# Output projection moved into the attention, head by head, on the chosen queries only

## The chip, the cores and the metric

One core of a Trainium2 chip runs the whole program in one launch. Its engines are TensorE (PE in the profile), VectorE (DVE), ScalarE (ACT), GpSimd (POOL) and SyncE (SP), which only issues DMAs. The metric is the device time of one execution in microseconds (us); less is better.

## The reference

The program is one transformer block with adaptive layer norm, on x of 4 batches of 2048 tokens with 512 features. The attention has 16 heads of 32 features, so there are 64 pairs of batch and head. Only the 409 queries of a head with the largest norm attend; all other token rows of that head are zero. What matters here:

```python
top_u = max(1, L // TOP_FACTOR)                       # 409 of 2048
_, top_idx = jax.lax.top_k(query_norms, top_u)
scores = jnp.einsum('bud,bld->bul', Q_sel, K) * scale
out_sel = jnp.einsum('bul,bld->bud', jax.nn.softmax(scores, axis=-1), V)
out_full = out_full.at[jnp.arange(BH)[:, None], top_idx].set(out_sel)   # zeros elsewhere
return out @ Wo.T + bo                                # per token: 512 -> 512
...
x = x + ga * attention(h)
h = layernorm(x) * (1 + cb) + sb
x = x + gb * ffn(h)      # 512 -> 1408 -> 512, both sides in blockwise FP4
```

## The kernel before

It runs in stages: `queries` and `keys_values` project the tokens and choose the queries (up to about 640 us), `attend` goes over the 64 heads (to about 1580 us), and `feed_forward` over 64 tiles of 128 tokens (to the end). There is no scheduler. Each engine has its program written out by hand as a list of steps with semaphore waits; in the middle each is a hardware loop (two heads or four tiles per turn), with the first and last turns written out.

In `attend`, a slot is one head on TensorE and has 8 steps k. Each step does `scores` (two 128x410 matmuls into one pair of PSUM banks), which ScalarE turns into exponentials; each odd step also does `weigh`, 8 fp32 matmuls with the values; each even step holds something smaller: a look for the row maxima of a coming head (`scores_for_max`), the transposes of queries (`turn_queries`), of maxima (`rows`) and of the output (`turn_output`). VectorE reduces the maxima and divides the output (`divide`). GpSimd, for each head, cuts the gathered queries into high and low halves (`cut_queries`), issues 4 indirect DMAs that gather the queries of the head two on, adds the bias bv, and issues 4 indirect DMAs (128, 128, 128 and 25 rows of 32 floats) that write the head's rows into the scratch tensor o_d (`scatter`). o_d has been filled with zeros before, a batch at a time.

In `feed_forward`, a tile's rows are loaded from o_d (a_in), transposed on TensorE (`turn_a`), split into f16 halves on ScalarE and VectorE (`high_of_a`, `low_of_a`), multiplied by Wo in 12 matmuls of 512 columns (`attention_out`), and taken with the bias bo on VectorE (`take_attention`). GpSimd then multiplies by ga and adds x (`residual`), VectorE and GpSimd normalise, modulate and quantise (`moments`, `normalise`, `modulate`, `quantise_h`, `scale_h`), and TensorE does the three products of the feed-forward with f16 halves (`gate_up`, `down`). `hidden_units`, `hidden_add` and `hidden_take` quantise the hidden 1408 values on VectorE, a tile behind. TensorE and VectorE work on three tiles at a time in a fixed order, `slot(t, ...)`.

Of the kernel before, what the change touches and what calls it, by code (L numbers as in the profile page):

```python
# [483 lines left out]
def keys_values(nc, keep, io, scratch, con, proj, h_hi, h_lo, early, ahead):  # L484
# [32 lines left out]
    with ExitStack() as stack:  # L517
# [5 lines left out]
        zeros = m.sb("zeros", [P, D], F32)  # L523
# [50 lines left out]
        bias_loaded, ones_set, zeros_set = keep.sem("bias_loaded"), keep.sem("ones_set"), keep.sem("zeros_set")  # L574
# [86 lines left out]
        with nc.Block() as block:  # L661
            @block.sync
            def _(sp):
# [53 lines left out]
                sp.dma_start(bv[:, :], io["bv"].unsqueeze(0).to_broadcast([P, D])).then_inc(bias_loaded, 16)  # L717
                for k in range(2):
                    sp.dma_start(nrm[k * BH:(k + 1) * BH, :], scratch["nrm"].rearrange("b h l -> (b h) l")[:, k * W:(k + 1) * W])\
                      .then_inc(nrm_loaded, 16)  # L720
# [5 lines left out]
                sp.wait_ge(zeros_set, 1)  # L726
# [5 lines left out]
                for s in range(BLOCKS):  # L732
# [16 lines left out]
                    if 1 <= s < 1 + PER_B:  # L749
                        sp.dma_start(o_blocks[s - 1], zeros[:, :].unsqueeze(1).to_broadcast([P, TB, D]))\  # L750
                          .then_inc(con["o_zeroed"], 16)
# [51 lines left out]
            def _(ve):  # L803
# [186 lines left out]
                ve.memset(v32[:, :, :, HD:VCOLS], 1.0).then_inc(ones_set, 1)  # L990
                ve.wait_ge(ones_set, 1)
                ve.sem_inc(v_done, TB)
                ve.memset(zeros[:, :], 0.0).then_inc(zeros_set, 1)
# [260 lines left out]
def attend(nc, keep, scratch, con, ffn, early, ahead, shared, banks, then):  # L1254
# [13 lines left out]
    ROWS_AT = 6  # L1268
    CHUNKS_AT = {0: ((1, 3), (1, 4)), 2: ((1, 5), (1, 6)), 4: ((2, 0),), 6: ((2, 1), (2, 2))}
    with ExitStack() as stack:  # L1270
# [9 lines left out]
        zeros = shared[:, at_o + QT * P:at_o + QT * P + D]  # L1280
# [3 lines left out]
        o_rows_of = [m.sb(f"o_rows{u}", [P, QT, HD], F32) for u in range(2)]  # L1284
        ps_max, ps_exp, ps_out, ps_misc = banks[0:2], *banks[2:5]

        o_pad, zeros_set = keep.sem("o_pad"), keep.sem("o_zeros_set")
# [10 lines left out]
        o_biased, o_stored = keep.sem("o_biased"), keep.sems("o_stored", 2)  # L1298
# [3 lines left out]
        o_rows = scratch["o"].rearrange("b l (h r) -> (b l h) r", r=HD)  # L1302
# [24 lines left out]
        with nc.Block() as block:  # L1327
            @block.sync
            def _(sp):

                f_front, f_run = then["sync"](sp, o_divided, o_stored)

                def load_k_max(h, u):
# [13 lines left out]
                def load_weights(k):  # L1347
                    part, w = divmod(k, 3)
                    if w < 2:
# [4 lines left out]
                def slot(i, u):  # L1354
# [3 lines left out]
                    if b + 1 < B and j < 8 and j % 2 == 0:  # L1358
                        sp.dma_start(o_blocks[b + 1, j // 2], zeros[:, :].unsqueeze(1).to_broadcast([P, TB, D])).then_inc(o_zeroed, 16)
# [5 lines left out]
                    if i == FRONT_IN:  # L1365
                        for v in range(2):
                            sp.wait_ge(o_stored[v], 16 * QT * H // 2)
                        f_front()

                for i in range(BH):  # L1370
                    if i == 4:
                        sp.wait_ge(zeros_set, 1)
                    slot(i, i % 2)
                f_run()
# [9 lines left out]
            def _(pool):  # L1384
                def scatter(h):
                    u = h % 2
                    pool.wait_ge(o_divided, h + 1)
                    pool.tensor_tensor(o_rows_of[u][:, :, :], o_rows_of[u][:, :, :],
# [3 lines left out]
                    if h % H == 0:  # L1392
                        pool.wait_ge(o_zeroed, 16 * (L // N) * (h // H + 1))
                    for t in range(QT):
                        n = rows_of(t, TOP)
                        pool.indirect_dma_start(o_rows, bass.IndirectOffsetOnAxis(ap=con["chosen"][0:n, t, h:h + 1], axis=0),  # L1396
                                                o_rows_of[u][0:n, t, :], None).then_inc(o_stored[u], 16)

                for h in range(BH):
# [4 lines left out]
                    if h >= 4:  # L1404
                        scatter(h - 4)
                f_constants, f_residual, f_modulate, f_scale_h, f_run = then["gpsimd"](pool)
                scatter(BH - 4)
                scatter(BH - 3)
# [4 lines left out]
                f_scale_h(0)  # L1413
                f_modulate(1, 0)
                scatter(BH - 2)
# [3 lines left out]
                scatter(BH - 1)  # L1419
# [928 lines left out]
```

## Time and profile before

| | |
|---|---|
| median of 3 runs | 3267.48 us (3266.4 to 3269.31) |
| the profiled execution's own time | 3266.15 us |
| its span, first to last instruction | 3264.3 us |
| TensorE busy | 3159.4 us (97%) |
| VectorE busy | 2544.5 us (78%) |
| ScalarE busy | 1143.1 us (35%) |
| GpSimd busy | 1562.5 us (48%) |

TensorE is busy nearly always, but its matmuls overlap in the records: a 512-column matmul is shown as 0.38 us and the next one starts 0.215 us after it. What a matmul costs is read from the distance between starts. Shares of busy time differ by stage, so each stage is looked at by itself.

### The profile page before, as it was taken

To read this page: it belongs to the slowest core of one execution; us is meant where nothing else is said; L and a number is where in the kernel's file an instruction comes from. 1 tells how busy PE (TensorE), PEld (TensorE's weight loads), DVE (VectorE), ACT (ScalarE), POOL (GpSimd) and SP (SyncE) were. 2 spreads that over 40 slices of the span, in tenths; PEclk is the share of its full clock that TensorE was granted. 3 is DMA by queue.
4 is the path that set the end of the run, shared out by engine and by line. 5 is a ranking of instruction groups with operands and counts; after the bars stand their busy time and mean duration, and the time that the engine had idled before them with its cause. 6 is when DMAs were issued, how large, how long until landed. Compare 5 with 4: busy or idle time off the path is not lost.

```text
span 3264.3 us, 49910 instructions
## 1 busy us (share of the span) xinstructions
PE 3159.4 (97%) x16684; PEld 1473.9 (45%) x16684; DVE 2544.5 (78%) x3769; ACT 1143.1 (35%) x1607; POOL 1562.5 (48%) x1420
## 2 busy tenths in 40 slices
PE   7998999899999999999999999999999999999998
PEld 3543454333333333333455555555555555555554
DVE  4657876566666666666789998998899999888995
ACT  6862323356666666665311111111111111111111
POOL 3432224266666666664544444444444444444442
PEclk9999999999999999999999999999999999999999
DMA  6856748655233343324110000110101000000000
GB/s 236 281 175 212 208 119 217 190 151 165 80 111 103 83 121 93 82 80 125 45 30 32 29 29 29 32 32 29 32 29 29 29 32 32 29 29 32 29 20 17
DMA packets 203480, 282.17 MB, mean 86 GB/s; under 512 B 59897, under 2 KB 115577, under 8 KB 202633
## 3 DMA queue, kind: packets, MB, share of 16 engines
q1 hardware_dynamic: 187016, 274.41, 27.8%
q0 software_dynamic: 16384, 6.76, 1.0%
q8 instruction: 43, 0.70, 0.1%
q14 instruction: 37, 0.30, 0.0%
HBM read 169.36 MB, written 111.70 MB: 86 GB/s over the span
## 4 chain that ended last, share of the span: by engine, by line
PE 74%; ACT 2%; DVE 2%; issue 1%; POOL 1%; DMA 0%; SPq 0%; ACTq 0%; POOLq 0%; DVEq 0%
PE bank L1648 12%; PE pair L2181 9%; PE pair L2183 9%; PE pair L2182 9%; PE pair L1637 7%; PE pair L1599 5%; PE bank L2203 4%; PE bank L2205 4%; PE bank L2204 4%; ACT shared L1540 2%; PE pair L2160 2%; PE pair L2162 2%; PE pair L2161 2%; PE bank L2193 1%; PE pair L2193 1%
## 5 line engine op out<-in xcount | busy, mean ns | idle before, releaser
L1435 DVE TENSOR_REDUCE top<-pair 128x1 f32<-128x1024 f32 x378 | 451.0, 1221 | 219.0 <-PE pair L1599 219.0
L1540 ACT ACTIVATE shared<-pair,p_bias 128x820 f32<-128x820 f32 x512 | 483.6, 945 | 369.7 <-PE pair L1637 369.6
L2181 PE MATMUL pair<-gu,xT_hi 128*128 128x512 f16 (+1 forms) x1536 | 555.0, 361 | 4.1 <-DVE bridge L1942 2.2
L2183 PE MATMUL pair<-gu,xT_lo 128*128 128x512 f16 (+1 forms) x1536 | 555.0, 361 | 0.0
L2182 PE MATMUL pair<-gu,xT_hi 128*128 128x512 f16 (+1 forms) x1536 | 555.0, 361 | 0.0
L1648 PE MATMUL bank<-shared,bridge 128*33 128x410 f32 x2048 | 404.8, 516 | 0.0
L1637 PE MATMUL pair<-q_exp,bridge 98*128 98x410 f16 x1024 | 267.6, 343 | 25.9 <-ACT shared L1540 25.4
L455 POOL DMA_INDIRECT q_sel<-q_d,chosen x256 | 245.8, 960 | 94.9 <-issue 79.0
L1396 POOL DMA_INDIRECT o_d<-o_rows,chosen x256 | 250.3, 978 | 81.5 <-issue 64.1
L2203 PE MATMUL bank<-dn,bridge 128*128 128x512 f16 x704 | 267.9, 381 | 0.0
L2204 PE MATMUL bank<-dn,bridge 128*128 128x512 f16 x704 | 267.8, 380 | 0.0
L2205 PE MATMUL bank<-dn,bridge 128*128 128x512 f16 x704 | 267.8, 380 | 0.0
L2113 ACT ACTIVATE silu<-pair 128x512 f32<-128x512 f32 (+1 forms) x128 | 69.6, 544 | 509.0 <-PE pair L2183 509.0
L1599 PE MATMUL pair<-bridge,q_max 96*128 96x512 f16 x756 | 209.0, 385 | 14.2 <-DVEq L1481 12.0
L2183 PEld LDWEIGHTS pair<-gu,xT_lo 128*128 128x128 f16 x1536 | 150.3, 98 | 153.9
L2181 PEld LDWEIGHTS pair<-gu,xT_hi 128*128 128x128 f16 x1536 | 150.3, 98 | 140.6 <-issue 3.5
L2182 PEld LDWEIGHTS pair<-gu,xT_hi 128*128 128x128 f16 x1536 | 150.3, 98 | 137.1
L2044 POOL TENSOR_SCALAR f_rstd<-f_mv 128x1 f32<-128x1 f32 x64 | 87.0, 1360 | 219.4 <-DVE f_mv L1915 219.4
L2107 ACT ACTIVATE xT_hi<-pair 128x512 f16<-128x512 f32 x64 | 38.2, 597 | 437.6 <-PE pair L2169 437.6
L1648 PEld LDWEIGHTS bank<-shared,bridge 128*33 128x33 f32 x2048 | 98.0, 110 | 204.2 <-issue 203.9
L1637 PEld LDWEIGHTS pair<-q_exp,bridge 98*128 98x128 f16 x1024 | 64.1, 97 | 264.7 <-ACT shared L1540 232.2
L2061 POOL TENSOR_TENSOR bridge<-bridge,q_scale 128x1408 f32<-128x1408 f32 x64 | 165.8, 2591 | 24.2 <-DVE bridge L1827 24.2
(280 smaller groups left out, 6036.9 us busy)
## 6 DMA issues: line engine op xcount, KB each, us to landing
bridge<-k_d SPq DMA_DIRECT2D x384, 128.0 KB, 3.3
v_d<-v SPq DMA_DIRECT2D x16, 1056.0 KB, 10.2
bridge<-v_d SPq DMA_DIRECT2D x64, 264.0 KB, 2.8
x<-in_x SPq DMA_DIRECT2D x16, 1024.0 KB, 8.6
q_d<-q SPq DMA_DIRECT2D x16, 1024.0 KB, 4.3
a_in<-o_d SPq DMA_DIRECT2D x64, 256.0 KB, 2.6
f_x<-in_x SPq DMA_DIRECT2D x64, 256.0 KB, 2.6
out<-shared SPq DMA_DIRECT2D x64, 256.0 KB, 2.0
```

Of the source, the lines that this page charges most:

```text
L1396: pool.indirect_dma_start(o_rows, bass.IndirectOffsetOnAxis(ap=con["chosen"][0:n, t, h:h + 1], axis=0), o_rows_of[u][0:n, t, :], None).the ...
L1435: ve.tensor_reduce(top[:, t, half:half + 1], ps[:, :, :].rearrange("p a n -> p (a n)"), AX.X, ALU.max, negate=True).then_inc(max_done, 1)
L1540: act.activation(p32[k % PB][:, :, :], ps_exp[:, :, 0:NQ], ACT.Exp, bias=con["p_bias"][:, 0:1], scale=scale).then_inc(p_done, 1)
L1599: last = pe.matmul(ps[:, s, :], q_max[u][:, t * P:(t + 1) * P], k_max[u][:, at:at + 512], start=True, stop=True)
L1637: last = pe.matmul(ps_exp[:, s, 0:NQ], k_exp[u][:, at:at + P], q_exp[u][:, :], start=True, stop=True)
L1648: last = pe.matmul(ps_out[at:at + VCOLS, 0:NQ], v_tok[u][:, t, :], p32[k % PB][:, s, :], start=k == 0, stop=k == STEPS - 1)
L2181: pe.matmul(o, xT_hi[:, c, :], w_hi[:, c, c0:c0 + n], start=c == 0, stop=False)
L2182: pe.matmul(o, xT_hi[:, c, :], w_lo[:, c, c0:c0 + n], start=False, stop=False)
L2183: last = pe.matmul(o, xT_lo[:, c, :], w_hi[:, c, c0:c0 + n], start=False, stop=c == KC - 1)
L2203: pe.matmul(ps_d[:, :], hT_hi[:, c, :], w_hi[:, c, :], start=c == 0, stop=False)
L2204: pe.matmul(ps_d[:, :], hT_hi[:, c, :], w_lo[:, c, :], start=False, stop=False)
L2205: last = pe.matmul(ps_d[:, :], hT_lo[:, c, :], w_hi[:, c, :], start=False, stop=c == FC - 1)
```

## The change

- In `attend`, each head's output is projected at once. After `divide`, GpSimd adds bv and cuts the result into f16 parts high, low, high (`cut_output`); TensorE transposes them (`turn_back`, 4 matmuls), VectorE copies them out (`take_back`), and TensorE multiplies by the 32 rows of Wo of that head, stacked as high, high, low (`project`, 4 matmuls with 96 rows of contraction and 512 columns). ScalarE scales the 4 results into SBUF (`take_rows`). They lie where dn[0], a half of the down weights, comes later.
- GpSimd's 4 indirect DMAs per head now add rows of 512 floats to whole token rows of o_d. Two heads can choose the same token, so the first of a head waits until all four of the head before have landed. The heads' steps trail: `divide` of a head is one slot behind TensorE's head, its `cut_output` too, its projections two and three slots behind.
- SyncE loads the head's rows of Wo (3 small DMAs, `load_wo`). o_d is filled with bo in place of zeros.
- In `feed_forward`, a_in is only loaded: `turn_a`, `high_of_a`, `low_of_a`, `attention_out` and `take_attention` are gone, and `residual` starts from a_in. `low_of_x` of the next tile moves ahead of `take_down`, and `turn_x` of the next tile into `down`. dn[0] is loaded after the last accumulating DMA has landed.

```diff
             def _(pool):
-                def scatter(h):
-                    u = h % 2
+                def scatter(h, tiles):
+                    for t in tiles:
+                        n = rows_of(t, TOP)
+                        pool.wait_ge(o_taken, h * QT + t + 1)
+                        if t == 0:
+                            for k in range(QT):
+                                need(pool, o_stored[k], 16 * h)
...
+                        pool.indirect_dma_start(o_rows, bass.IndirectOffsetOnAxis(ap=token[0:n, t, h:h + 1], axis=0),
+                                                o_tile[t][0:n, :], None, compute_op=ALU.add).then_inc(o_stored[t], 16)
+
+                def cut_output(h):
                     pool.wait_ge(o_divided, h + 1)
...
+                    need(pool, o_back, h)
+                    pool.tensor_copy(o_split[:, :, :].rearrange("p t (k r) -> p t k r", k=3)[:, :, 0:3:2, :],
+                                     o_div[:, :, :].unsqueeze(2).to_broadcast([P, QT, 2, HD])).then_inc(o_high, 1)
+                    pool.wait_ge(o_high, h + 1)
+                    pool.tensor_tensor(o_split[:, :, HD:2 * HD], o_div[:, :, :], o_split[:, :, 0:HD], ALU.subtract).then_inc(o_cut, 1)
+
+                def outputs(h):
+                    if 0 <= h - 2:
+                        scatter(h - 2, range(1, QT))
+                    if 0 <= h < BH:
+                        cut_output(h)
+                    if 0 <= h - 1 < BH:
+                        scatter(h - 1, range(1))
...
             def _(act):
+                def take_rows(h, t, bank):
+                    n = rows_of(t, TOP)
+                    act.wait_ge(o_proj, h * QT + t + 1)
+                    need(act, o_stored[t], h * 16)
+                    act.activation(o_tile[t][0:n, :], bank[0:n, :], ACT.Copy, scale=1.0 / (W_UP * O_UP)).then_inc(o_taken, 1)
...
             def _(pe):
+                def project(h, u, t, bank, loaded, taken):
+                    n = rows_of(t, TOP)
...
+                    pe.matmul(bank[0:n, :], oT[u][:, t * P:t * P + n], wo_head[u][:, :], start=True, stop=True).then_inc(o_proj, 1)
...
         def residual(t, t4, b):
-            hold(pool, y_done, t + 1, pool_held)
-            pool.tensor_tensor(y[:, :], y[:, :], vec["ga"][:, b, :], ALU.mult).then_inc(ga_done, 1)
+            pool.wait_ge(fa_in[t4 % 2], in_turn(t, t4))
+            if has(t, -1):
+                hold(pool, x2_done, t, pool_held)
+            pool.tensor_tensor(y[:, :], a_in[t4 % 2][:, :], vec["ga"][:, b, :], ALU.mult).then_inc(ga_done, 1)
...
         def slot(t, t4, b1, b2, b_z):
             hidden(t, 1)
-            if has(t, 2):
-                low_of_a(t + 2)
             if has(t, 1):
                 quantise_h(t + 1)
             hidden(t, 2)
             hidden_units(t)
+            if has(t, 1):
+                low_of_x(t + 1)
             if has(t, -2):
                 take_down(t - 2, b_z)
```

TensorE in the attention loop, from the scores of an odd step to those of the next one, first before and then after (`wo_head,oT` is a projection, `o_split` the transposes of `turn_back`, `shared,bridge` the weighing):

```order
L1637 MATMUL pair<-q_exp,bridge 128x410 x2
L1648 MATMUL bank<-shared,bridge 33x410 x2
L1648 MATMUL bank<-shared,bridge 33x410 x2
L1637 MATMUL pair<-q_exp,bridge 128x410 x2
L1599 MATMUL pair<-bridge,q_max 128x512 x2
L1603 MATMUL pair<-bridge,q_max 26x512 x4
L1637 MATMUL pair<-q_exp,bridge 128x410 x2
```

```order
L1701 MATMUL pair<-q_exp,bridge 128x410 x2
L1712 MATMUL bank<-shared,bridge 33x410 x2
L1744 MATMUL bank<-wo_head,oT 128x512
L1712 MATMUL bank<-shared,bridge 33x410 x2
L1701 MATMUL pair<-q_exp,bridge 128x410 x2
L1661 MATMUL pair<-bridge,q_max 128x512 x2
L1665 MATMUL pair<-bridge,q_max 26x512 x4
L1734 MATMUL bank<-ident,o_split 96x128 x3
L1734 MATMUL bank<-ident,o_split 96x26
L1701 MATMUL pair<-q_exp,bridge 128x410 x2
```

A projection stands between the two halves of each odd step's weighing, four to a head, and the four transposes at the end of step 2.

GpSimd in the attention, one head and the start of the next, before and after (`q_sel<-q_d` gathers the queries, `o_d<-` writes or adds the output rows):

```order
L465 CAST q_split<-q_sel 128x4x64
L468 TENSOR_TENSOR q_split<-q_sel,q_split 128x4x32
L455 DMA q_sel<-q_d,chosen 128x32 x3
L455 DMA q_sel<-q_d,chosen 26x32
L1388 TENSOR_TENSOR o_rows<-o_rows,bv 128x128
L1396 DMA o_d<-o_rows,chosen 131072x32 x4
```

```order
L465 CAST q_split<-q_sel 128x4x64
L468 TENSOR_TENSOR q_split<-q_sel,q_split 128x4x32
L455 DMA q_sel<-q_d,chosen 128x32 x3
L455 DMA q_sel<-q_d,chosen 26x32
L1415 DMA o_d<-dn,token 8192x512 x3
L1420 TENSOR_TENSOR o_div<-o_div,bv 128x128
L1425 CAST o_split<-o_div 128x4x2x32
L1428 TENSOR_TENSOR o_split<-o_div,o_split 128x4x32
L1415 DMA o_d<-dn,token 8192x512
```

The number of DMAs is the same; three of an older head now stand ahead of the addition of bv and one behind the cut, and that one waits for the three.

VectorE in the feed-forward loop, over the boundary between two tiles, before and after (`bank,shared` is `take_down`, `xT_lo` is `low_of_x`, `pair,bo` is `take_attention`, the 1408 wide ones are `hidden_add`):

```order
L1812 SCALAR_TENSOR_TENSOR bridge<-bridge,q_inv 128x1408
L1956 SCALAR_TENSOR_TENSOR bridge<-bank,shared 128x512
L1895 TENSOR_TENSOR xT_lo<-pair,xT_hi 128x512
L1948 SCALAR_TENSOR_TENSOR bridge<-bank,bridge 128x512
L1908 SCALAR_TENSOR_TENSOR bridge<-pair,bo 128x512
L1948 SCALAR_TENSOR_TENSOR bridge<-pair,bridge 128x512
L1819 TENSOR_SCALAR bridge<-bridge 128x1408
```

```order
L1918 SCALAR_TENSOR_TENSOR bridge<-bridge,q_inv 128x1408
L1999 TENSOR_TENSOR xT_lo<-pair,xT_hi 128x512
L2047 SCALAR_TENSOR_TENSOR bridge<-bank,shared 128x512
L2039 SCALAR_TENSOR_TENSOR bridge<-bank,bridge 128x512
L2039 SCALAR_TENSOR_TENSOR bridge<-pair,bridge 128x512
L1925 TENSOR_SCALAR bridge<-bridge 128x1408
```

`take_attention` has gone, and `low_of_x` and `take_down` have changed places.

## Rows read from the trace of the kernel before

**Rows 1.** Busy time by stretch: length, PE, PEld, DVE, ACT, POOL, clock, DMA share.

```profile
700.00:1510.00 810.00, 789.50 (x4413) 269.00 (x4413) 553.79 (x964) 500.88 (x623) 505.36 (x619) 1.00 0.37 106
1700.00:3100.00 1400.00, 1400.00 (x7312) 733.64 (x7310) 1261.24 (x1559) 228.10 (x430) 667.24 (x485) 1.00 0.10 30
```

**Rows 2.** Instructions in order of time, PE, attention: start us, length us, [idle before].

```profile
1070.88 0.47 PE L1585 MATMUL bank<-ident,q_split 128*96 128x128 f16 x4
1071.29 1.04 PE L1599 MATMUL pair<-bridge,q_max 96*128 96x512 f16 x4
1072.16 0.52 PE L1637 MATMUL pair<-q_exp,bridge 98*128 98x410 f16 x2
1072.61 1.57 PE L1648 MATMUL bank<-shared,bridge 128*33 128x410 f32 x8
1074.12 0.52 PE L1637 MATMUL pair<-q_exp,bridge 98*128 98x410 f16 x2
...
1075.75 0.52 PE L1637 MATMUL pair<-q_exp,bridge 98*128 98x410 f16 x2 [0.35 <-ACT shared L1540]
...
1085.20 0.47 PE L1585 MATMUL bank<-ident,q_split 128*96 128x128 f16 x4
```

**Rows 3.** The same of GpSimd, attention.

```profile
1069.08 0.98 POOL L1396 DMA_INDIRECT o_d<-o_rows,chosen  x1 [0.30 <-issue]
1070.37 0.97 POOL L1396 DMA_INDIRECT o_d<-o_rows,chosen  x1 [0.30 <-issue]
...
1072.58 0.40 POOL L465 CAST q_split<-q_sel 128x256 f16<-128x256 f32 x1
...
1077.63 0.89 POOL L455 DMA_INDIRECT q_sel<-q_d,chosen  x1 [0.30 <-issue]
1081.44 0.45 POOL L1388 TENSOR_TENSOR o_rows<-o_rows,bv 128x128 f32<-128x128 f32 x1 [2.92 <-DVE o_rows L1470]
```

**Rows 4.** DMA issues, whole span: count, KB each, median us to landing.

```profile
a_in<-o_d SPq DMA_DIRECT2D x64, 256.0 KB, 2.6
...
out<-shared SPq DMA_DIRECT2D x64, 256.0 KB, 2.0
```

**Rows 5.** In order of time, PE, feed-forward.

```profile
2401.16 0.38 PE L2160 MATMUL pair<-wo_hi,aT_hi 128*128 128x512 f16 x1
...
2403.75 0.60 PE L2193 MATMUL pair<-ident,bridge 128*128 128x128 f32 x4
...
2414.88 0.60 PE L2154 MATMUL pair<-ident,a_in 128*128 128x128 f32 x4
...
2427.21 0.38 PE L2160 MATMUL pair<-wo_hi,aT_hi 128*128 128x512 f16 x1
```

**Rows 6.** In order of time, VectorE, feed-forward.

```profile
2402.09 0.68 DVE L1956 SCALAR_TENSOR_TENSOR bridge<-bank,shared 128x512 f32<-128x512 f32 x1
...
2405.63 1.22 DVE L1819 TENSOR_SCALAR bridge<-bridge 128x1408 int32<-128x1408 int32 x1
...
2408.76 1.62 DVE L1823 TENSOR_TENSOR bridge<-bridge 128x1408 f32<-128x1408 f32 x1
...
2417.09 0.69 DVE L1805 TENSOR_REDUCE q_amax<-f_h 128x32 f32<-128x512 f32 x1
...
2427.80 0.68 DVE L1956 SCALAR_TENSOR_TENSOR bridge<-bank,shared 128x512 f32<-128x512 f32 x1
```

**Rows 7.** In order of time, GpSimd, feed-forward.

```profile
2402.86 1.27 POOL L2067 TENSOR_TENSOR shared<-x,bridge 128x512 f32<-128x512 f32 x1 [4.21 <-DVE bridge L1956]
2404.83 1.27 POOL L2036 TENSOR_TENSOR bridge<-bridge,vec_ga 128x512 f32<-128x512 f32 x1 [0.71 <-DVE bridge L1908]
2406.17 1.80 POOL L2040 TENSOR_TENSOR x<-f_x,bridge 128x512 f32<-128x512 f32 x1
...
2415.78 1.27 POOL L2050 TENSOR_TENSOR f_h<-f_h,vec_sb 128x512 f32<-128x512 f32 x1 [0.18 <-POOL f_h L2048]
```

**Rows 8.** VectorE near the end, where GpSimd is idle.

```profile
3212.46 0.88 DVE L1819 TENSOR_SCALAR bridge<-bridge 128x1408 int32<-128x1408 int32 x1
```

**Rows 9.** ScalarE, a copy of 512 columns out of PSUM.

```profile
2409.65 0.60 ACT L2113 ACTIVATE silu<-pair 128x512 f32<-128x512 f32 x1 [4.66 <-PE pair L2183]
```

More of the change, by code:

```diff
@@ L1418, in _ @@
                 f_modulate(2, 0)
-                scatter(BH - 1)
+                scatter(BH - 2, range(1, QT))
+                scatter(BH - 1, range(QT))
                 f_run()
@@ L1594, in scores_for_max @@
                     need(pe, max_done, h * CH + c - 1)
+                    if c == 1 and (not isinstance(h, int) or h >= 4):
+                        pe.wait_ge(o_taken, (h - 4) * QT + 1)
                     ps = ps_max[(u + c) % 2]
@@ L1738, in feed_forward @@
     res = late[0:2]
-    (ps_w, t0), (g0, u0), (g1, u1) = ((pair[:, 0, :], pair[:, 1, :]) for pair in banks[0:3])
+    (_, t0), (g0, u0), (g1, u1) = ((pair[:, 0, :], pair[:, 1, :]) for pair in banks[0:3])
     ps_d, t1 = banks[3][:, :], banks[4][:, :]
@@ L1868, in slot @@
                 load_vector(5, "gb")
-        def scattered():
-            for u in range(2):
-                sp.wait_ge(stored[u], 16 * QT * BH // 2)
+                for k in range(QT):
+                    sp.wait_ge(stored[k], 16 * BH)
+                sp.dma_start(ffn["dn"][0][:, :, :], scratch["dn"][0]).then_inc(con["f_in"], 16)
         def last():
@@ L1960, in slot @@
             if at(t, 0):
-                take_attention(2)
-                hidden(0, 0)
                 moments(2, 2)
@@ L1965, in slot @@
                 hidden(0, 1)
-                low_of_a(3)
                 hidden(0, 2)
@@ L1983, in slot @@
                 ve.wait_ge(vec_in["gb"], 16)
-            else:
-                low_of_x(t)
             if has(t, -2):
                 low_of_hidden(t - 2, 0)
-            if has(t, 1):
-                take_attention(t + 1)
             if has(t, -2):
@@ L2023, in run @@
             drive(ve, slot, last)
-        return low_of_a, take_attention, moments, normalise, quantise_h, low_of_x, run
+        return hidden, moments, normalise, quantise_h, low_of_x, run
     def gpsimd(pool):
@@ L2131, in slot @@
             gate(t, 1)
-            if at(t, 0):
-                high_of_a(3)
-            elif has(t, 2) and not at(t, 1):
-                high_of_a(t + 2)
             gate(t, 2)
@@ L2195, in turn_hidden, with down @@
             last.then_inc(t_turned, 1)
-        def down(t):
+        def down(t, turn=None):
             need(pe, z_done, t)
+            if at(t, 0):
+                pe.wait_ge(con["f_in"], 6 * 16)
             for k, (c0, n) in enumerate(T2_CHUNKS):
+                if k == 2 and turn is not None:
+                    turn_x(turn)
                 pe.wait_ge(t_lo, turn2_at(t, k) + 1)
@@ L2220, in slot @@
             if at(t, 2):
-                attention_out(3)
-                pe.wait_ge(divided, BH)
+                pe.wait_ge(projected, BH * QT)
             if has(t, -2):
                 turn_hidden(t - 2, 0)
-            if has(t, 1) and not at(t, 2):
-                attention_out(t + 1)
             if has(t, -2):
@@ L2232, in slot @@
             gate_up(t, 1)
-            if has(t, 2):
-                turn_a(t + 2, t4 + 2)
             gate_up(t, 2)
             if has(t, -2):
-                down(t - 2)
+                down(t - 2, t + 1 if has(t, 1) else None)
         def last():
```

275 lines of the change are left out of this document (155 added, 120 removed).

## The prediction

> **What bounds the kernel now.** I first read the busy time by stretch. The attention and the feed-forward are both TensorE's: 789.5 of 810 us and 1400 of 1400 us [rows 1]. Then the instructions in order of time, for the length of a turn. In the attention a head takes 1085.20 - 1070.88 = 14.32 us [rows 2], with one wait of 0.35 us for an exponential; VectorE and ScalarE stand at 68% and 62%, GpSimd at 62% and more, since about 0.3 us lie between its issues [rows 1, 3]. In the feed-forward a tile takes 2427.21 - 2401.16 = 26.05 us [rows 5]. There VectorE is at 90% [rows 1]: 1261.24/1400 of 26.05 us is 23.5 us. So the change adds to the engine that bounds the attention, and takes from the engine that bounds the feed-forward, but a second engine stands right behind it there.
>
> **What the attention pays.** TensorE, per head:
> - 4 projections. Four 512-column matmuls took 1072.16 - 1071.29 = 0.87 us, so one is 0.22 us. Each stands inside the fp32 weighing, and going from f16 into fp32 costs something: the two 410-column scores take 0.45 us before the weighing [rows 2], where 2 x 410 columns at 0.87/2048 us each would be 0.35 us. With 0.09 to 0.10 us for it, a projection costs 0.31 us, four 1.25 us. Bounds: 0.22 us each (0.87), and 0.40 us each if the fp32 pipeline drains at both sides (1.6).
> - 4 transposes of `turn_back`. Their like took 1071.29 - 1070.88 = 0.41 us. They stand at the end of step 2, just where TensorE waited 0.35 us for the exponential [rows 2], so 0.02 to 0.06 us are left.
>
> That is 1.27 us, a head of 15.6 us. ScalarE gets 4 copies of 0.60 us [rows 9]: 62% of 14.32 is 8.9 us, plus 2.4 is 11.3 of 15.6 us. They come right behind an odd step's exponential, and the next scores are then still 0.75 us of weighing away, so they delay no exponential. VectorE gets one copy of 410 columns, under 0.7 us by its 512-column operations [rows 6], on 9.8 us. Both are hidden while TensorE is the bound.
>
> GpSimd has the same 8 indirect DMAs, at 1070.37 - 1069.08 = 1.29 us each, and two more operations, like its cast of 0.40 us [rows 3]. 8 x 1.29 + 0.9 (cut of the queries) + 1.6 (bias and cut of the output, with gaps) is 12.9 us of 15.6. The new wait is the thing: the first scatter of a head waits until the four of the head before have landed. Behind it in GpSimd's queue stand the next cut of the queries and four gathers, then three scatters. From the start of a head's last scatter round to the next one's: its issue 1.0 us, landing, the first scatter 1.29, cut and gathers 1077.63 - 1072.58 + 1.28 = 6.3, two scatters 2.6: 11.2 us plus the landing. While it is under 15.6 - 11.2 = 4.4 us from the end of the issue, TensorE never sees it. No row shows an accumulating DMA. 256 KB read from o_d landed in 2.6 us and 256 KB written took 2.0 us [rows 4]; the accumulate must read and write, so 2.0 us is the floor and 4.6 us one after the other, and above that there is no row: sharing the queues with the loads of keys could double it, to 9 us. I take 3.5 us, between the two sums, also because the last of the four has only 25 rows. The issue itself may be longer than 1.29 us too, as each row needs another read; at 1.6 us the free landing shrinks to about 3 us.
>
> The Trainium skill (DMA: Bandwidth & Descriptors, Anatomy of one DMA) gives 2.0 us plus bytes over 436 GB/s for a DMA issued from GpSimd; an estimate by it is 2.6 us for 128 rows of 2 KB, which would leave the wait hidden. No run here shows it for an accumulating one.
>
> About 62 slots carry this: 62 x 1.27 = +79 us (54 to 100 by the bounds, with the wait hidden).
>
> **What the feed-forward gives back.** TensorE loses 12 matmuls, 2403.75 - 2401.16 = 2.6 us, and four transposes, under 0.6 us [rows 5]: it needs 23.0 us a tile. If that were all, 58 tiles would give 177 us. It isn't, since VectorE and GpSimd form a ring that takes nearly as long as before. I follow it from `take_down` to `take_down`, 2427.80 - 2402.09 = 25.71 us in this tile [rows 6]:
> - `low_of_a` goes, 0.68 us. But the next operation, q_amax at 2417.09, started when GpSimd's last modulation ended (2415.78 + 1.27 = 2417.05) [rows 6, 7]. VectorE now waits there instead; nothing is gained.
> - `take_attention` goes, and with it GpSimd no longer waits for it (0.71 us idle ahead of 2404.83). GpSimd's three additions now follow each other from 0.77 us after `take_down`. VectorE comes to `hidden_add` at 2.06 us instead of 3.54 us, into these. The two engines do not run such operations together: L1819 took 1.22 us here and 0.88 us where GpSimd is idle [rows 6, 8], and GpSimd's addition 1.80 us, where its like takes 1.27. Taken in turn: 0.77 + 1.27 + 1.27 + 0.76 + 1.15 + 0.76 = 5.98 us from `take_down` to L1823. Before it was 2408.76 - 2402.09 = 6.67 us, but that held `low_of_x` (0.60 us), which now comes at the other end of the ring.
> - So the ring is 5.98 + (25.71 - 6.67) + 0.60 = 25.6 us; with the handovers as short as the trace has them, 25.4. I take 25.5, against 26.05: 0.55 us a tile, times 58 is -32 us.
>
> Bounds: if GpSimd's additions and `hidden_add` fell beside each other for nothing, the ring would lose 0.7 to 0.9 us more, 24.6 us (-84 us); if they fell worse, 26.05 (0). The rule behind it is in the Trainium skill (SBUF — State Buffer, two separate sides): the port pair that VectorE and GpSimd share is an exclusive lock held for the whole instruction. By this rule the trace agrees, with 1.22 against 0.88 us, and it speaks against the change: work that is taken off VectorE next to GpSimd's additions turns partly into waiting for them.
>
> **The rest.** Between the stages GpSimd now issues 4 x 4 scatters among the first tiles' modulations, with waits for landings; TensorE was short of work there already. 0 to 20 us, I take 5. The load of the down weights waits for the last scatter, but its first use comes two tiles (some 29 us) after the last projection. The load of bo and the smaller SyncE steps hide behind loads that run anyway: 0 to 2, I take 0.
>
> Sum, against the execution profiled: 3266.15 + 79 - 32 + 5 = 3318. The median shown is 1.3 us above that execution, which is nothing here.
>
> **Rivals.**
> 1. GpSimd's ring binds the attention: slower still. Place: the wait for the four landings ahead of a head's first scatter; it decides from a landing of 4.4 us on (3 us if an issue takes 1.6 us), and each us more costs 62 us. At 6 us: 17.2 us a head, 3318 + 99 = 3417; at 8 us some 3540. For it: the loads of keys share the engines at 37% [rows 1]; against it: 25 rows only in the last scatter, and 4.6 us as the sum of a read and a write.
> 2. The feed-forward falls to TensorE's 23.0 us: faster. It needs VectorE's waits for GpSimd to vanish. 3266 + 79 - 177 + 5 = 3173. Against it: 23.5 us of VectorE's own work less 1.3 is 22.2, and the waits for GpSimd's reciprocal root and modulations, which stay, are 2 us on top.
> 3. The two cancel: projections at 0.22 us and a ring of 24.6 to 25 us. 3266 + 55 - 60 to -84 + 5 = 3242 to 3266.
>
> **Chances.** The forecast as worked out (3285 to 3350): 0.52. Rival 1: 0.25. Rival 2: 0.08. Rival 3: 0.15, of which half within 0.2% (6.5 us, about what a measurement here can tell from none). So faster 0.16, same 0.08, slower 0.76. The range reaches from rival 3's lower part to rival 1 with a landing of 6 us: 3245 to 3420; the forecast's own is 3285 to 3350.
>
> **What would show it.** Right: a head of 15.4 to 15.7 us with projections spaced 0.31 us inside the weighing, GpSimd idle ahead of the first scatter; a tile of 25.2 to 25.7 us, TensorE waiting in it for low_of_x or hidden, q_amax waiting over 1 us for GpSimd, L1819's successor at 1.5 us or more. Wrong: TensorE waiting in the attention for ScalarE's copies or GpSimd (rival 1), or a tile of 23 us (rival 2).

## The result, and the profile after

The changed kernel takes 3469.0 us (median of 4 runs, 3464.34 to 3475.03), the kernel before 3268.23 us beside it: a ratio of 1.0619 (1.0605 to 1.0632), 201 us slower. The profiled execution has a span of 3466.3 us, against 3264.3: 202.0 us more, which the traces divide as follows. The bounds are instructions that both kernels have: the transposes of a head's output in TensorE's timeline (L1659 before, L1725 after) and q_amax<-f_h on VectorE, once a tile.

| stretch | before, us | after, us | difference | the prediction had |
|---|---|---|---|---|
| up to head 0's output | 678.0 | 674.5 | -3.5 | 0 |
| head 0 to head 59 (59 heads) | 844.8 | 1045.3 | +200.5 | +79 (62 heads) |
| head 59 to tile 3 | 113.3 | 143.3 | +30.0 | +5 |
| tile 3 to tile 63 (60 tiles) | 1562.4 | 1536.4 | -26.0 | -32 (58 tiles) |
| tile 63 to the end | 65.8 | 66.8 | +1.0 | 0 |

First the page of the changed kernel: the span, the queue that the indirect transfers use (packets, MB, share of 16 engines), and the costliest lines that are new.

```profile
span 3466.3 us, 50118 instructions
PE 3179.1 (92%) x16172; PEld 1385.0 (40%) x16172; DVE 2527.9 (73%) x3706; ACT 1266.6 (37%) x1799; POOL 1792.8 (52%) x1548
q0 software_dynamic: 41984, 57.03, 11.9%
L1415 POOL DMA_INDIRECT o_d<-dn,token x256 | 400.4, 1564 | 275.0 <-DMA o_d<-dn,token 125.7
L455 POOL DMA_INDIRECT q_sel<-q_d,chosen x256 | 246.7, 964 | 94.2 <-issue 59.4
```

The scatter that adds takes GpSimd 1564 ns to issue, the gather beside it 964. The same stretches as in [rows 1], and the attention's as before:

```profile
700.00:1510.00 810.00, 760.42 (x3899) 233.42 (x3898) 467.51 (x818) 506.19 (x680) 550.45 (x584) 0.96 0.65 137
1900.00:3300.00 1400.00, 1291.49 (x6564) 647.55 (x6565) 1240.85 (x1475) 211.02 (x383) 702.82 (x494) 1.00 0.10 31
```

TensorE is no longer busy all the time in either. In the attention its granted clock is 0.96 where it was 1.00, and the DMA engines' share of busy time has gone from 0.37 to 0.65.

Now TensorE in order of time, a head without a wait. It answers to [rows 2], where eight fp32 matmuls stood in one piece:

```profile
704.93 0.50 PE L1725 MATMUL bank<-ident,shared 97*128 97x97 f32 x4
...
705.89 0.88 PE L1712 MATMUL bank<-shared,bridge 128*33 128x410 f32 x4
706.70 0.39 PE L1744 MATMUL pair<-wo_head,oT 96*128 96x512 f16 x1
707.02 0.88 PE L1712 MATMUL bank<-shared,bridge 128*33 128x410 f32 x4
707.84 0.52 PE L1701 MATMUL pair<-q_exp,bridge 98*128 98x410 f16 x2
...
721.05 0.50 PE L1725 MATMUL bank<-ident,shared 97*128 97x97 f32 x4
```

This head is 721.05 - 704.93 = 16.12 us. From the weighing's start to the next score it is 707.84 - 705.89 = 1.95 us; before it was 1074.12 - 1072.61 = 1.51 us [rows 2]. A projection costs 0.44 to 0.45 us, of which 0.32 are its own distance (706.70 to 707.02) and 0.12 lie in the two halves of the weighing, 0.81 and 0.82 us instead of 1.51 for both.

But the heads are not all 16.12 us. Their mean is 1045.3 / 59 = 17.72. GpSimd in order of time shows why:

```profile
1069.27 1.62 POOL L1415 DMA_INDIRECT o_d<-dn,token  x1 [0.30 <-ACT dn L1594]
1071.20 1.57 POOL L1415 DMA_INDIRECT o_d<-dn,token  x1 [0.30 <-issue]
1073.07 1.47 POOL L1415 DMA_INDIRECT o_d<-dn,token  x1 [0.30 <-issue]
...
1078.85 1.59 POOL L1415 DMA_INDIRECT o_d<-dn,token  x1 [2.85 <-DMA o_d<-dn,token]
...
1085.48 0.90 POOL L455 DMA_INDIRECT q_sel<-q_d,chosen  x1 [0.31 <-issue]
1086.68 1.62 POOL L1415 DMA_INDIRECT o_d<-dn,token  x1 [0.30 <-issue]
1088.61 1.57 POOL L1415 DMA_INDIRECT o_d<-dn,token  x1 [0.30 <-issue]
1090.48 1.46 POOL L1415 DMA_INDIRECT o_d<-dn,token  x1 [0.30 <-issue]
...
1096.40 1.60 POOL L1415 DMA_INDIRECT o_d<-dn,token  x1 [3.00 <-ACT dn L1594]
```

A scatter stands 1.9 us before the next (1.29 in [rows 3]). From a head's first scatter to the end of its last is 1090.48 + 1.46 - 1078.85 = 13.1 us, then comes the landing: 1078.85 - (1073.07 + 1.47) = 4.3 us. This is one turn; in the 51 turns of the steady part the first piece is 13.1 us each time, and the second goes from 3.4 to 6.6. In 34 turns a landing ends it (4.5 us on average), in the other 17, but for two, ScalarE's copy of a projected row tile (4.9 us), as in the last row above. 13.1 + 4.5 = 17.6 us is longer than TensorE's 16.12, and everything that hangs on a landing hands the wait on. ScalarE's copy into the row tile waits for the head before to land; TensorE's transposes of the next queries, in the bank that this copy empties, wait for ScalarE:

```profile
1075.11 0.60 ACT L1594 ACTIVATE dn<-bank 128x512 f32<-128x512 f32 x1 [2.73 <-DMA o_d<-dn,token]
```
```profile
1075.76 0.51 PE L1645 MATMUL bank<-ident,q_split 128*96 128x128 f16 x4 [1.53 <-ACT dn L1594]
```

TensorE's waits for these copies add up to 60 us in the 59 heads. That is not all of the 94 us by which the heads exceed TensorE's own (1045.3 less 59 x 16.12). In 14 of the 59 the granted clock fell as well, to a mean of 0.84 to 0.92 over the head, and 30 us of their length lie neither in the 16.12 nor in their waits. The drop comes behind a long wait. In the head that starts at 1029.35 us TensorE waits 2.96 us, and then stands at 0.50, the lower of its two levels (1.2 GHz, not 2.4):

```profile
1040.25 0.51 PE L1645 MATMUL bank<-ident,q_split 128*96 128x128 f16 x4 [2.96 <-ACT dn L1594]
```
```profile
1042.00:1044.00 2.00, 2.00 (x6) 0.30 (x5) 0.69 (x1) 0.94 (x1) 0.96 (x1) 0.50 0.00 0
```

GpSimd's turns average 17.72 us, as long as the heads, and the turns that end with a landing need 17.6, so the ring sets the pace. What TensorE lost to the clock can have added little to it: for the most part it lies in time that TensorE would otherwise have waited.

In the feed-forward a tile is 25.61 us. VectorE in one of them, against [rows 6]:

```profile
2400.90 0.69 DVE L1911 TENSOR_REDUCE q_amax<-f_h 128x32 f32<-128x512 f32 x1 [1.40 <-POOL f_h L2136]
2401.62 1.83 DVE L1914 TENSOR_SCALAR q_scale<-q_amax 128x32 f32<-128x32 f32 x1
...
2414.28 1.96 DVE L1925 TENSOR_SCALAR bridge<-bridge 128x1408 int32<-128x1408 int32 x1
2416.28 1.84 DVE L1927 TENSOR_SCALAR bridge<-bridge 128x1408 f32<-128x1408 f32 x1
```

q_amax waits 1.40 us for GpSimd's modulation, and L1925 takes 1.96 us beside GpSimd's additions, where its predecessor took 1.22, and 0.88 alone [rows 6, 8]. TensorE waits three times in that tile, for xq, for xT_lo (1.02 us) and for hidden; these are two:

```profile
2412.36 0.66 PE L2254 MATMUL pair<-ident,bridge 128*128 128x128 f32 x4 [1.02 <-DVE xT_lo L1999]
...
2424.29 0.32 PE L2242 MATMUL pair<-gu,xT_hi 128*128 128x384 f16 x1 [0.59 <-DVE bridge L2033]
```

Between the stages, from head 59 to tile 3, TensorE waits 36.1 us where it waited 10.3 before. 14.7 us of it are for ScalarE's copies of projected rows (dn), 5.7 for oT, the copy that VectorE makes of the turned output; these two waits are new:

```profile
1779.67 0.88 PE L1725 MATMUL bank<-ident,shared 97*128 97x97 f32 x4 [5.68 <-DVE oT L1506]
...
1824.78 0.60 PE L1744 MATMUL bank<-wo_head,oT 96*25 96x512 f16 x1 [10.50 <-ACT dn L1594]
```

In the second ScalarE itself waited 10.51 us for a scatter to land, and GpSimd had issued that scatter at 1818.99 us, behind tile 2's residual and modulation.

### The profile page after: what moved, and what is told of

The parts are those of the page before. It is cut to its first block, busy times and chain, and to the rows that moved or that the text cites. A ratio compares the mean times of both kernels' runs of the same rounds, so it can differ in the third digit from the quotient of the medians.

```text
span 3466.3 us, 50118 instructions
## 1 busy us (share of the span) xinstructions
PE 3179.1 (92%) x16172; PEld 1385.0 (40%) x16172; DVE 2527.9 (73%) x3706; ACT 1266.6 (37%) x1799; POOL 1792.8 (52%) x1548
## 3 DMA queue, kind: packets, MB, share of 16 engines
q0 software_dynamic: 41984, 57.03, 11.9%
## 4 chain that ended last, share of the span: by engine, by line
DVE 24%; POOL 20%; issue 13%; PE 13%; DMA 8%; ACT 2%; POOLq 0%; SPq 0%; DVEq 0%; ACTq 0%
DMA o_d<-dn,token 8%; POOL o_d L1415 5%; POOL q_sel L455 5%; DVE q_scale L1914 3%; PE bank L1712 3%; DVE bridge L1927 3%; DVE q_amax L1911 3%; POOL f_rstd L2130 3%; DVE bridge L1925 2%; POOL f_h L2134 2%; POOL f_h L2136 2%; PE pair L1701 2%; PE pair L1661 1%; DVE q_inv L1916 1%; DVE q_xn L1918 1%
## 5 line engine op out<-in xcount | busy, mean ns | idle before, releaser
L1415 POOL DMA_INDIRECT o_d<-dn,token x256 | 400.4, 1564 | 275.0 <-DMA o_d<-dn,token 125.7
L1712 PE MATMUL bank<-shared,bridge 128*33 128x410 f32 x2048 | 468.3, 538 | 0.0
L1661 PE MATMUL pair<-bridge,q_max 96*128 96x512 f16 x756 | 223.2, 391 | 17.8 <-DVEq L1523 12.1
L2141 POOL TENSOR_TENSOR q_xq<-q_xn,q_scale 128x512 f32<-128x512 f32 x64 | 68.8, 1075 | 227.9 <-DVE q_xn L1933 227.9
```

The costliest lines, as they stand in the source:

```text
L1712: last = pe.matmul(ps_out[at:at + VCOLS, 0:NQ], v_tok[u][:, t, :], p32[k % PB][:, s, :], start=k == 0, stop=k == STEPS - 1)
```

## Experiments

The stretches named below are those of the table. Each experiment ran on one chip together with the kernel before, and its ratio is to that. e1 to e8 fell on chips where the kernel before takes 3266 to 3267 us; the later ones where it took longer, of which more under e10.

### e1 and e2: what the accumulate costs

e1 leaves out the addition and writes the rows plainly, e2 leaves out half of each row.

```diff
-   o_tile[t][0:n, :], None, compute_op=ALU.add)          # e1
+   o_tile[t][0:n, :], None)
-   o_rows = scratch["o"].rearrange("b l d -> (b l) d")   # e2
+   o_rows = scratch["o"].rearrange("b l (k d) -> (b l k) d", k=2)
-   o_tile[t][0:n, :], None, compute_op=ALU.add)
+   o_tile[t][0:n, 0:D // 2], None, compute_op=ALU.add)
```

> The 256 indirect DMAs that add head rows into the token rows write them instead (same rows, same bytes, same waits; so what is loaded at the end is not the sum). Theory A (the accumulate makes GpSimd's ring too long: issue every 1.93 us instead of 1.29 us, landing some 4.5 us): the issue falls back to 1.29 us, the landing to 2 to 3 us, the ring to about 14 us, under TensorE's 16.12 us a head. Then every head takes 16.12 us and about 100 us go: 3360 to 3380 us. Rival B (the ring is long because the key loads share the DMA queues, accumulate or not): the landing stays above 4 us and at most 30 us go, 3440 us or more. Rival C (the longer heads come from the granted clock or from ScalarE's copies, not from the scatters): no change, 3469.

> The accumulating DMAs move 256 of each row's 512 numbers (the same count of rows, half the bytes; the other half of the sum is left out). If the cost of the accumulate is per row (a descriptor and a read each), the issue stays at 1.9 us spacing and the landing falls by less than 1 us: 3430 to 3469 us. If it goes by bytes, the landing falls by 1.5 to 2 us: the ring is 15.5 us and under TensorE's 16.12, 3360 to 3400 us.

e1: 3362.7 us, ratio 1.0297 (1.0280 to 1.0314): 106 us less than the changed kernel. Heads 0 to 59 take 949.5 us, 16.09 each. e2: 3383.6 us, 1.0361 (1.0344 to 1.0378), 85 us less, heads of 16.33 us. Three rows say what happened, the first of e1's page:

```profile
L1415 POOL DMA_INDIRECT o_d<-dn,token x256 | 252.7, 987 | 173.3 <-ACT dn L1594 106.0
```

and two of GpSimd in e2:

```profile
1002.50 1.46 POOL L1415 DMA_INDIRECT o_d<-dn,token  x1 [0.30 <-issue]
...
1006.74 1.59 POOL L1415 DMA_INDIRECT o_d<-dn,token  x1 [1.32 <-DMA o_d<-dn,token]
```

A plain write of the same rows is issued in 987 ns. With half the bytes the accumulate is issued as slowly as before (1564 ns mean), but lands 1006.74 - 1003.96 = 2.8 us after the issue instead of 4.3. So the bytes don't set the issue, and the landing falls with them. The rows don't set the issue either: the fourth scatter of a head has 25 rows and takes 1.46 us, the others have 128 and take 1.57 to 1.62. Nearly all of it is a price for each DMA. Theory A holds; its rivals B and C are out, since the addition alone was removed and all heads fell to TensorE's length at a granted clock of 1.00. Of e2's two answers the first was right on the issue, though not on its reason, and the second on the landing and the time.

### e3 and e4: the ring, and the place of the projections

```diff
-                    if 0 <= h - 2:                        # e3, e4
-                        scatter(h - 2, range(1, QT))
+                    if 0 <= h - 2:
+                        scatter(h - 2, range(QT))
                     if 0 <= h < BH:
                         cut_output(h)
-                    if 0 <= h - 1 < BH:
-                        scatter(h - 1, range(1))
-                            weigh(i, u, k - 3, in_turn(i, u, 0))   # e4 only
-                            project_in_turn(i, u, k)
+                            project_in_turn(i, u, k)
+                            weigh(i, u, k - 3, in_turn(i, u, 0))
                             weigh(i, u, k - 2, in_turn(i, u, 0))
```

> A head's first scatter is moved on GpSimd from behind the cut of the output to stand directly ahead of the other three, so that the landing of the four passes beside the cuts and the gathers and not in a wait. Theory A: GpSimd's turn is then 4 x 1.93 + 4 x 1.29 + about 2.5 = 15.4 us with no landing in it, TensorE's 16.12 us bounds every head: 3360 to 3380 us. Rival D (the indirect DMAs are held up in the queues themselves, so that GpSimd only waits elsewhere): less than 40 us go.

> As the one before, and each projection on TensorE is moved from between the two fp32 weighings of a step to ahead of both, behind the f16 scores. Theory A (a projection costs 0.45 us in the place it has: 0.22 us of columns and 0.23 us for leaving and entering fp32 once more): TensorE's head is 15.2 us; GpSimd's 15.4 us is then about as long: 3300 to 3330 us. Rival E (the 0.23 us belongs to the projection wherever it stands): as the one before.

e3: 3371.0 us, 1.0321 (1.0304 to 1.0338). The same operations with the same waits, in another order, and the heads are 16.12 us one like the other (949.5 us for 59); 98 us of the 201 are gone. So a wait goes away when GpSimd has other issues to make meanwhile, and rival D is out. The granted clock is back as well. Its stretch as in [rows 1], and below it e4's:

```profile
700.00:1510.00 810.00, 809.51 (x4322) 256.58 (x4321) 513.25 (x902) 564.36 (x755) 610.57 (x653) 1.00 0.68 149
```
```profile
700.00:1510.00 810.00, 806.41 (x4505) 286.13 (x4503) 537.21 (x946) 564.61 (x785) 636.39 (x680) 1.00 0.74 155
```

e4: 3334.2 us, 1.0210 (1.0193 to 1.0227), heads of 15.42 us. Ahead of the weighing, behind the f16 scores, a projection costs (15.42 - 14.32) / 4 = 0.28 us at most, in the middle of it 0.45. Theory A had 15.2 us for TensorE and 15.4 for GpSimd. The 15.42 are TensorE's own: in all of the 59 heads it waits for 3.0 us in total.

### e5 to e8: a remedy that was none

```diff
-        ve.tensor_scalar(sc[:, :], am[:, :], 1.0 / 6.0, 1e-12, ALU.mult, ALU.max).then_inc(step, 1)   # e5, e6, e7, e8
+        ve.scalar_tensor_tensor(out=sc[:, :], in0=am[:, :], scalar=1.0 / 6.0, in1=tiny[:, 0:1].to_broadcast([P, nb]),
+                                op0=ALU.mult, op1=ALU.max).then_inc(step, 1)
...
-                f_residual(2, 2, 0)                                            # e8
-                f_modulate(2, 0)
                 scatter(BH - 2, range(QT))
+                f_residual(2, 2, 0)
+                f_modulate(2, 0)
```

> The changed kernel with one VectorE instruction in another form: L1914 (q_scale<-q_amax, 128x32 and 128x88) is a scalar_tensor_tensor with a constant as second operand instead of a tensor_scalar with two numbers. In the trace of the changed kernel the 128x32 one takes 1.83 us wherever GpSimd's L2147 (2.58 us) runs, and 0.18 us elsewhere. Theory F (the feed-forward is bounded by the ring of VectorE and GpSimd, and this is a wait for GpSimd inside it): the tile falls from 25.61 us by about 1.6 us to 24.0, times 60: 3370 us (3360 to 3385). Rival G (TensorE is the bound again, or VectorE waits for GpSimd a few operations later instead): tile 25.3 us or more, 3450 to 3469 us.

> The same edit in the kernel before. There TensorE has no idle time in a tile of 26.04 us. If TensorE bounds it, nothing changes but the transition: 3255 to 3267 us. If VectorE and GpSimd bounded it in truth: 24.4 us a tile, about 3170 us.

> The changed kernel with the scatters together, the projections first, and q_scale unlocked. By the sums so far: 3334 from the first two, less 97 us of theory F: 3237 us (3225 to 3250), under the kernel before. If theory F fails, 3320 or more.

> As the one before, and between the stages GpSimd issues the scatters of head 62 ahead of tile 2's residual and modulation, not behind them. TensorE waited 6.89 us there for ScalarE, which waited for these to land. If that wait is what makes the transition long: 5 to 8 us less than the one before. If another wait takes its place (tile 2's quantisation comes later by the four issues, 7.5 us): the same or up to 5 us more.

e5: 3470.9 us, 1.0623 (1.0602 to 1.0645), tile 25.66 us: nothing. Theory F's remedy failed, but not as rival G had it either. The row of e5:

```profile
2402.04 1.84 DVE L1915 SCALAR_TENSOR_TENSOR q_scale<-q_amax,f_tiny 128x32 f32<-128x32 f32 x1
```

The other form stands still just as long, 1.84 us, to the end of GpSimd's scaling of the hidden row (2401.24 + 2.59 = 2403.83 us). The Trainium skill says that itself (SBUF — State Buffer, Who interferes with whom): a VectorE instruction with two inputs in SBUF contends with a GpSimd one that reads SBUF, and tensor_reduce never does. The trace agrees in both: q_amax, a reduction that starts at 2401.32 us beside the same GpSimd operation, keeps its 0.69 us.

e6 (the kernel before with the edit): 3267.7 us, 1.0001 (0.9991 to 1.0010), as TensorE's bound wants it, though after e5 it could show nothing else. e7 is e4 with this edit, e8 is e7 with head 62's scatters moved ahead of tile 2's work on GpSimd. e7: 3336.5 us and e8: 3335.5 us, both as e4. In e8 TensorE's longest wait for ScalarE's copy is 3.99 us instead of 5.49, and its wait for tile 2's xT_lo 4.62 instead of 2.42: the one took the place of the other.

### e9 and e10: the feed-forward's ring

```diff
             if has(t, 1):                       # GpSimd; e9, e10
+                gated(t + 1, t4 + 1, b1)        # y = a_in * ga, no longer inside residual
             if has(t, -3):
                 result(t - 3, t4 + 1)
...
-            if has(t, -1):                      # GpSimd; e10
-                scale_hidden(t - 1)
             if has(t, 1):
                 scale_h(t + 1)
+            if has(t, -1):
+                scale_hidden(t - 1, t4 + 1)
...
-            hidden_units(t)                     # VectorE; e10: q_amax, q_scale, q_inv,
-            low_of_x(t + 1)                     # then low_of_x, then the scaling L1918
+            hidden_units(t, t4, lambda: low_of_x(t + 1))
```

> The kernel with the scatters together and the projections first (e4, 3334 us), and in the feed-forward GpSimd's multiplication by ga (L2122, 1.27 us) is taken from behind the final addition (L2153) to ahead of it, where GpSimd stood idle for 4.8 us. Theory H (the tile is a ring in which VectorE's L1925 and L1927 stand still while GpSimd's three additions and multiplications run): they wait 1.0 us less, the tile falls from 25.61 to 24.6 (24.3 to 24.9), times 60: 3275 us (3255 to 3290). Rival I (the wait moves to the next place, as with q_scale in e5): tile 25.5 or more, 3325 us or more.

> As the one before, and GpSimd scales the hidden row (L2147, 2.58 us) behind scale_h instead of ahead of it, with low_of_x on VectorE ahead of the scaling L1918 of 1408 columns and two buffers for the hidden q_scale. Then q_amax is followed by q_scale at once and GpSimd's 2.58 us lie beside VectorE operations that did not wait in the traces (L1911, L1999). Theory H: 1.65 us less of standing still, but TensorE's own 23.5 us a tile is the floor: tile 23.6 to 24.2 us, 3215 to 3245 us, under the kernel before. Rival I: the tile stays at that of the run before.

e10 also gives the hidden q_scale a second buffer, which the lines above leave out. The tile fell to 24.76 us in e9 and 24.09 us in e10, as theory H had it; rival I is out. Four VectorE rows of e10:

```profile
2405.06 1.68 DVE L1913 TENSOR_SCALAR q_scale<-q_amax 128x88 f32<-128x88 f32 x1
...
2411.27 1.07 DVE L1927 TENSOR_SCALAR bridge<-bridge 128x1408 int32<-128x1408 int32 x1
...
2422.69 0.69 DVE L1909 TENSOR_REDUCE q_amax<-f_h 128x32 f32<-128x512 f32 x1 [1.40 <-POOL f_h L2140]
2423.41 0.18 DVE L1913 TENSOR_SCALAR q_scale<-q_amax 128x32 f32<-128x32 f32 x1
```

The small q_scale is back at 0.18 us (1.83 in the changed kernel) and the first operation of `hidden_add`, on 1408 columns, at 1.07 (1.96). But the hidden q_scale now stands still, 1.68 us where it took 0.21: a part of the wait moved. TensorE is busy for 1347.65 of 1400 us in that stage, where the changed kernel had 1291.49.

The times were 3377.3 us (1.0156, 1.0140 to 1.0171) and 3340.0 us (1.0048, 1.0035 to 1.0061), not the 3275 and 3215 to 3245 expected: there the kernel before took 3323.4 us, and heads 0 to 59 of the new version 1006 us where e4 had 912.

### e11 to e17: other chips

> The kernel of e10 again. In e10's call the kernel before itself took 3323 us instead of 3267, and heads of the attention 16.9 us where e4 had 15.42 at the same instructions. If that belongs to the chip, e10's tile of 24.09 us gives here, beside a kernel before of 3267 us, 3334 - 60 x (25.61 - 24.09) = 3243 us (3230 to 3255), ratio 0.990 to 0.996. If the longer heads are caused by the edits in the feed-forward (which lie behind the attention), it is 3330 us or more again.

> The kernel of e4 again, beside e11 on one chip, so that the difference of the two is the feed-forward's edits alone: e11 plus 60 x 1.52 = 91 us (80 to 100).

e11: 3339.2 us, 1.0037 (1.0024 to 1.0049). e12, which is e4 again: 3437.4 us, 1.0330 (1.0308 to 1.0353), with heads of 17.23 us, in a kernel that ran with 15.45 before. So the longer heads do not come from the edits but from where and when the kernel ran, and the feed-forward's edits are worth 98 us (80 to 100 expected). The attention of this version is hit harder there than that of the kernel before. The chip alone need not be it: e9 and e10 ran on chip 7, with 3323.4 us for the kernel before, and e13 to e15 on chip 7 too, with 3301.2.

> The version of e10 and e11, and on VectorE the moments, normalisation and quantisation of tile 0 stand behind the copy of head 61's turned output (take_back in head 63's turn) and not ahead of head 63's turn. TensorE waited 4.0 us in e4 and 5.7 us in the changed kernel for that copy (oT L1506). Theory J (VectorE's place in tile 0 makes that wait): it goes, the passage from head 59 to tile 3 is 3 to 6 us shorter than in e15. Rival K: tile 0 comes later by as much and TensorE waits for xT_lo instead: within 2 us of e15.

> The kernel before, unchanged, for its trace on this chip. If the chip is like the first: 3264 to 3270 us with heads of 14.32 us. If it is the one of the last two calls: about 3324 us, and the 57 us stand in the attention (heads of 15.2 us, 0.9 us more, with ScalarE waiting once a head), the tile at 26.04 us.

> The version of e10 and e11. On a chip like the first: 3234 to 3245 us, ratio 0.990 to 0.994. On the other chip: 3340 us, ratio 1.004.

The edit of e13 moves four steps in VectorE's program (f_moments(0, 0) to f_moments(1, 1)) from the end of head 62's turn to behind take_back of head 63's. e13: 3341.8 us, 1.0127 (1.0108 to 1.0145), e15: 3330.1 us, 1.0087 (1.0073 to 1.0102). The wait for oT went and one of 12.31 us for ScalarE's exponential came a few steps on; the passage from head 59 to tile 3 took 145.4 us against 137.9. The version without this edit has 132.5, 141.4, 137.9 and 141.2 us there in its four traces (e10, e11, e15, e16), so single traces differ by 9 us and say no more than this: nothing was gained. Theory J failed, and K, which had it within 2 us and with a wait for xT_lo, is not shown either. e14 took 3297.8 us, with heads of 14.87 us instead of 14.32 and the tile at 26.04. Its attention, to be read beside [rows 1]:

```profile
700.00:1510.00 810.00, 764.08 (x4248) 259.28 (x4244) 535.83 (x929) 482.86 (x599) 491.00 (x599) 1.00 0.36 103
```

> The version of e10, e11 and e15. On a chip where the kernel before takes 3267 us: heads of 15.4 us, tiles of 24.1 us, 3235 to 3250 us, ratio 0.990 to 0.995. On a chip where it takes 3300 us or more: ratio 1.004 to 1.009 as so far.

> The changed kernel with only the projections moved ahead of both weighings; GpSimd's order is left. TensorE's own head is 0.7 us shorter. If the ring (13.1 us plus a landing of 4.5 us = 17.6 us) bounds every head, at most 10 us go. If TensorE's 16.12 us bounds the heads between the waits, as the heads of exactly 16.12 us in the changed kernel suggest, part of the 59 x 0.7 = 41 us goes: 15 to 30 us, ratio to the kernel before 1.053 to 1.058.

e16: 3333.3 us, 1.0102 (1.0085 to 1.0119), on a chip where the kernel before took 3299.1 us. e17: 3498.0 us, 1.0607 (1.0589 to 1.0625), heads of 18.20 us. That is not shorter than the ring's 17.6. But the changed kernel itself was not run there, and even e16, with its scatters together, has heads of 17.07 us, so e17 proves nothing; e1 and e3 do.

On a chip like the first the best version would be e4 less 60 x (25.61 - 24.09) = 91 us, 3243 us, 0.7% under the kernel before. That is an estimate, not measured; measured four times (e10, e11, e15, e16), always where the kernel before took 3299 us or more, it was 0.4 to 1.0% slower. No version measured here beats the kernel before.

## Why the prediction was wrong

- **The step that failed** is "While it is under 15.6 - 11.2 = 4.4 us ..., TensorE never sees it": GpSimd's ring was put at 11.2 us plus a landing, and the wait at nothing. It was +94 us above TensorE's own head (200.5 less 59 x 1.80), and (17.72 - 15.6) x 59 = 125 us above the forecast's. The landing was not far off, 4.5 us against 3.5 and inside the bounds. The issue was: 1.29 us was taken over from a plain scatter, 1.9 was measured, and the fallback named (1.6) was still too short. The four scatters make the 11.2 us 13.1, which leaves 16.12 - 13.1 = 3.0 us for a landing of 4.5. Neither error alone would have done much: 13.1 + 3.5 = 16.6 and 11.2 + 4.5 = 15.7 us, against 16.12. Rival 1 named this place and mechanism, with 0.25; the sign that it gave for itself, TensorE waiting for ScalarE's copies, is what the trace shows. But its sums let only the landing grow, and its 3417 us at a landing of 6 us falls short for that reason. No term stood for the clock either: 60 of the 94 us are TensorE's waits and 30 lie in the 14 heads in which its clock fell behind one. e1 and e3 take away both together and can't part them. e3 takes away the wait and leaves the dearer issue, and gives back 98 us; e1 takes away the dearer issue and landing, and gives back 106.
- **Projections on TensorE**: 0.31 us each was right for the distance to the next matmul (0.32) and wrong for the cost, 0.45. The working had only the way from f16 into fp32; that the weighing's halves on both sides become longer (0.12 us) was left out. The bounds had 0.40 "if the fp32 pipeline drains at both sides"; even this was passed. The head of a TensorE without waits is 16.12 us, not 15.6: 59 x 1.80 = +106 us, against 59 x 1.27 = 75. e4 shows that the place costs it.
- **`turn_back`, ScalarE, VectorE in the attention**: hidden, as said. ScalarE's copies did come into the chain, but as carriers of the landing.
- **The feed-forward**: 25.61 us a tile where 25.5 was taken, -26 us for 60 tiles where the forecast's rate gives -33. The working by VectorE's and GpSimd's ring held in both parts, so this was not luck: from `take_down` to L1823's successor it had 5.98 us, and the trace has 2418.15 - 2412.22 = 5.93, which leaves 19.68 for the rest of the ring where it had 19.64; q_amax waits 1.40 us for GpSimd, L1925 takes 1.96 us. e9 and e10 show that the ring was the bound, since reordering it (in e10 with one more buffer) gave 0.85 and 1.5 us a tile. TensorE's own work is 1291.49/1400 of 25.61 = 23.6 us, not 23.0. Rival 2 was rightly low.
- **Between the stages**: +5 was too small, +30 measured (bound: 20). TensorE's waits grew by 36.1 - 10.3 = 26 us there, most of all for ScalarE's copies, which waited for landings. The 5 us had left this chain out, though it is the one of the attention. With plain writes the stretch is 130.1 us and TensorE waits 25.1 us in it, so by single traces some 13 of the 30 come from the accumulate. Four heads fall in it, 4 x 1.80 = 7 us more. What would remove the rest is open: e8 and e13 each removed one wait, and another came in its place.

In the sum, with -2.5 for the two ends: 106 + 94 + 30 - 26 - 2.5 = 201.5 us, against 202.0 between the spans. The projections' error alone would have left the time in the range (3318 + 31 + 25 = 3374 us). The ring's would not: at 17.6 us a head it lies above TensorE's head whether that is 15.6 or 16.12 us, so in the changed kernel it is the bound, and the +106 became the bound only once e3 had taken the ring away.

## What to carry to other kernels

An operation that no trace shows (here a scatter that adds) has two prices, what it costs the engine that issues it and how long it is away; bound each for itself, and put both into the ring it closes. If an engine must wait for its own transfer, put its other issues between the issue and the wait: this order alone was worth 98 us of 3469 here. And an f16 matmul is better placed beside f16 matmuls: here it cost 0.28 us there and 0.45 us inside a group of fp32 ones.

## What the runs showed of the hardware

- An indirect DMA that adds is issued by GpSimd in 1564 ns, a plain one of the same 2 KB rows in 987 (e1); with rows of 1 KB it stays at 1564 (e2), and with 25 rows instead of 128 it falls only to 1460. The last of four (25 rows in it, the others 128) had landed 4.3 us after its issue with 2 KB rows, 2.8 us with 1 KB.
- The adding transfers take the DMA engines longer than their bytes say: queue 0 moves 57.03 MB at a share of 11.9% of the engines' span, 57.02 MB as plain writes at 4.9% (e1), and 30.23 MB of half rows at 6.9% (e2).
- One kernel's time differs by place and occasion: the kernel before took 3266 to 3269 us beside e1 to e8 and the changed kernel, and 3299 to 3325 beside e9 to e17, in e14's trace all of it in the attention (14.87 us a head). The version of e4 lost 1.8 us a head there (e12).
- What it lost is mostly a wait. In e10 TensorE waits 76 us in the 59 heads, nearly all for ScalarE's exponential and some 1.3 us at a time, where e4 has 3.0 us; in 11 of the heads its clock also fell to 0.50, the lower level, behind such a wait. The wait is gone behind GpSimd's last gather: in all seven traces of these versions (e9 to e13, e15, e16) the last two of the 59 heads take 15.37 to 15.43 us, as in e4. Whether it is the gathers that matter, and why there and not in e4, is open. TensorE in one head of e10, and the busy times by stretch behind it:

```profile
1049.18 0.86 PE L1699 MATMUL pair<-q_exp,bridge 98*128 98x410 f16 x2 [1.43 <-ACT shared L1580]
```
```profile
1050.00:1052.00 2.00, 2.00 (x8) 0.57 (x9) 1.44 (x5) 1.41 (x2) 1.54 (x2) 0.50 1.09 242
```
